# Attention that begins inside the layer norm, routing cut into pieces, pair rows staged from device memory

## The reference, cut to what matters

```python
# x: [4, 1024, 256] float32; 16 heads of 16; 8 experts, hidden 1024, top 2
xn = (x - mean(x)) / sqrt(var(x) + 1e-5)
q, k, v = xn @ W_q.T, xn @ W_k.T, xn @ W_v.T
decay[h, i, j] = gamma[h] ** (i - j) if i >= j else 0
attn = einsum('bihd,bjhd->bhij', q, k) * decay / sqrt(16)      # no softmax
y = einsum('bhij,bjhd->bihd', attn, v)
yn = (y - mean_h(y)) / sqrt(var_h(y) + eps)                    # over tokens and head dims
attn_out = (yn * gn_weight + gn_bias) @ W_o.T
probs = softmax(xn @ gate_w.T + gate_b)                        # [4096, 8]
val, idx = top_k(probs, 2)
ffn_out = sum_k val[k] * (relu(xn @ w1[idx[k]] + b1[idx[k]]) @ w2[idx[k]] + b2[idx[k]])
out = x + attn_out + ffn_out
```

## Time and profile before

| what | us |
|---|---|
| median of 3 runs | 790.35 |
| lowest, highest | 789.27, 793.92 |
| the profiled execution, its own time | 788.52 |
| its span, first to last instruction | 786.7 |
| first scores of attention in it | 61.6 |
| last round of attention in it ends near | 276 |

### The profile page before, as it was taken

How to read it: one execution, slowest core, us unless ns; L and a number is a source line. 1 busy time by engine, 2 the same in 40 slices (tenths; PEclk the granted TensorE clock), 3 DMA queues, 4 the chain that set the end, 5 groups by cost and what they waited for, 6 DMA issues and landing times.

```text
span 786.7 us, 20206 instructions
## 1 busy us (share of the span) xinstructions
PE 732.9 (93%) x6588; PEld 678.4 (86%) x6588; DVE 584.2 (74%) x1024; ACT 498.2 (63%) x880; POOL 283.1 (36%) x225
## 2 busy tenths in 40 slices
PE   2948999999999988999999999999999999999967
PEld 1426788888887788999999999999999999999957
DVE  6776777777777776877877878777778778778545
ACT  3832334333333386787787787887877877877780
POOL 0013333333334313344344354353353453443420
PEclk9977999999999998999999999999999999999988
DMA  9995333333334485788888888788888888886249
GB/s 294 371 335 176 119 105 108 98 103 101 101 101 136 157 299 150 227 218 252 213 232 251 206 236 257 184 250 242 208 247 239 213 249 227 217 252 173 35 109 332
DMA packets 89047, 157.85 MB, mean 201 GB/s; under 512 B 26496, under 2 KB 66560, under 8 KB 78976
## 3 DMA queue, kind: packets, MB, share of 16 engines
q1 hardware_dynamic: 74720, 138.87, 53.8%
q0 software_dynamic: 14304, 18.69, 14.5%
HBM read 111.67 MB, written 37.37 MB: 189 GB/s over the span
## 4 chain that ended last, share of the span: by engine, by line
PE 85%; DVE 5%; issue 4%; ACT 2%; DMA 2%; POOL 0%; SPq 0%; POOLq 0%; ACTq 0%; DVEq 0%; another core or an unknown queue 0%
PE ps L744 28%; PE ps L648 27%; PE ps L704 6%; PE ps L773 6%; PE ps L717 3%; PE ps L796 3%; PE ps L760 2%; PE ps L908 2%; PE ps L729 2%; PE ps L784 2%; PE ps L666 1%; PE ps L754 1%; PE ps L807 1%; ACT arena_f L539 1%; DMA xn<-x 1%
## 5 line engine op out<-in xcount | busy, mean ns | idle before, releaser
L648 PE MATMUL ps<-arena_r 128*128 128x256 f32 x1872 | 235.2, 286 | 2.2 <-DVE arena_r L1184 2.2
L744 PE MATMUL ps<-arena_r 128*128 128x256 f32 x1872 | 233.4, 285 | 1.9 <-DVE arena_r L1101 1.1
L744 PEld LDWEIGHTS ps<-arena_r 128*128 128x128 f32 x1872 | 229.5, 194 | 2.4 <-issue 2.4
L648 PEld LDWEIGHTS ps<-arena_r 128*128 128x128 f32 x1872 | 228.3, 193 | 2.4 <-issue 2.4
L444 POOL TENSOR_TENSOR fence_out<-eps_col 128x1 f32<-128x1 f32 x39 | 78.7, 2019 | 274.6 <-DVE arena_f L1160 274.6
L498 ACT ACTIVATE arena_r<-arena_f 128x2048 fp32r<-128x2048 f32 x77 | 143.7, 1921 | 0.0
L446 POOL DMA_INDIRECT sum_rows<-arena_f,pair_slot x78 | 122.7, 1574 | 18.1 <-issue 17.3
L580 ACT ACTIVATE arena_f<-ps,arena_f 128x256 f32<-128x256 f32 x156 | 65.3, 471 | 90.5 <-PE ps L744 79.5
L1176 DVE TENSOR_TENSOR arena_r<-arena_f,arena_r 128x2048 fp32r<-128x2048 f32 x39 | 89.4, 2292 | 38.7 <-ACT arena_r L498 38.7
L1184 DVE TENSOR_TENSOR arena_r<-arena_f,arena_r 128x512 fp32r<-128x512 f32 x78 | 55.9, 717 | 53.7 <-ACT arena_r L588 51.9
L1084 DVE TENSOR_TENSOR arena_f<-ps,cst 128x512 f32<-128x512 f32 x128 | 84.7, 683 | 14.9 <-PE ps L773 14.9
(11 more groups left out here) (134 smaller groups left out, 855.2 us busy)
## 6 DMA issues: line engine op xcount, KB each, us to landing
arena_f<-w SPq DMA_DIRECT2D x78, 1024.0 KB
xs_rows<-spare_rows SPq DMA_DIRECT2D x39, 258.0 KB, 3.6
arena_f<-xs_rows SPq DMA_DIRECT2D x39, 258.0 KB, 3.8
pair_chunk<-xn SPq DMA_DIRECT2D x32, 256.0 KB, 2.6
arena_f<-b SPq DMA_DIRECT2D x39, 128.0 KB, 4.0
xn<-x SPq DMA_DIRECT2D x8, 512.0 KB, 8.8
x_chunk<-xn SPq DMA_DIRECT2D x32, 128.0 KB
arena_f<-sum_rows SPq DMA_DIRECT2D x8, 512.0 KB, 7.6
```

The source lines that it names most:

```text
L648: last = pe.matmul(out_ap, lhs(a), rhs(b), start=start and n == 0, stop=stop and n == 2, **kw)
L744: last = pe.matmul(ps[:, H_BANK[hp], o * SLOT:(o + 1) * SLOT], w1_r[par][:, a, at:at + P], xs_r[:, b, k * SLOT:(k + 1) * SLOT], start=(m = ...
```

## The change

It has these parts.

1. **Loads.** SP loads group 0, the identity alone, group 1, gate weights, W_k and W_v, group 2, W_q, the other constants, groups 3 to 7, bias, W_o, gn.
2. **Layer norm.** Groups are normalised in place in `xn`: two tiles by VectorE, one by ScalarE, one by GpSimd; the copy back is gone. The gate's weights are padded to 32 columns so that the four tiles' logits go to four column blocks of TensorE (eight matmuls of 128 columns for two of 512), and one matmul brings a group's logits back. VectorE adds the bias once, for all groups, in round 0 of attention.
3. **Attention's head.** x_transposes(0) follow group 3, the first projections group 5. scores(0) no longer wait for routing.
4. **Routing in pieces.** VectorE does shifted_logits in round 1, and so on to experts_of_slots in round 11, each between new_state and the masked scores. The two counting matmuls are in round 5. Probabilities come from two exponentials and one sum. output_stats of the first rounds are left out there and done two a round in rounds 12 to 21.
5. **Pair rows.** SP writes each normalised group to `xn_rows` in device memory, with two spare-row writes between two groups; the other 25 spare rows follow three a round, the x copy in step 10. From step 11 on SP stages two tiles a step from `xn_rows`, with two DMAs each, into four buffers; the indirect DMAs read their rows from `rows2`. The first expert weights are issued in step 27. SP's and GpSimd's rounds are written out, without a loop. `y_t` waits for `xn_out` in place of a staging.

The diff, cut to its core:

```diff
@@ sync
             ln_load(0)
-            sp.dma_start(cst[:], const).then_inc(s["consts_in"], 16)
...
+            sp.dma_start(cst[:, 0:P], const[:, 0:P]).then_inc(s["ident_in"], 16)
+            ln_load(1)
+            sp.wait_ge(s["gate_zero"], 1)
...
+            weights_in(0)
+            ln_load(2)
+            weights_in(1)
+            sp.dma_start(cst[:, P:], const[:, P:]).then_inc(s["consts_in"], 16)
+            for g in range(3, NG):
+                ln_load(g)
...
+            def rows_out(g):
+                for name in ("ln_xn_v", "ln_xn_a", "ln_xn_p"):
+                    sp.wait_ge(s[name], g + 1)
+                sp.dma_start(xn_rows[:, g * GRP:(g + 1) * GRP, :], xn[:, g * GRP:(g + 1) * GRP, :]).then_inc(s["xn_out"], 16)
...
+            def pairs_stage(n):
+                b = n % NPB
+                wait(sp, s[f"scat{b}"], n // NPB * 32)
+                sp.dma_start(pair_chunk[b][:, :, 0:D], xn_rows[:, n:n + 1, :].to_broadcast([P, 2, D])).then_inc(s[f"rc{b}"], 16)
+                sp.dma_start(pair_chunk[b][:, :, D:W], pair_info[:, n]).then_inc(s[f"rc{b}"], 16)
+
+            rows_out(0)
             tokens_stage(0, 0)
             tokens_stage(1, 1)
             sp.wait_ge(s["spare"], 1)
...
+            for g in range(1, NG):
+                spare_out(2 * g - 2)
+                spare_out(2 * g - 1)
+                rows_out(g)
             sp.wait_ge(s["xt_psum"], 1)
             tokens_stage(2, 0)
...
+            def chunk_step(i):
+                if i + 3 < NT:
+
+                    sp.wait_ge(s["xt_psum"], i + 2)
+                    tokens_stage(i + 3, (i + 3) % 2)
+                for sl in range(2 * NG - 2 + 3 * i, min(2 * NG - 2 + 3 * i + 3, NS)):
+                    spare_out(sl)
+                if i == PAIRS_AT - 1:
+                    sp.dma_start(sum_rows[0:NT * P].rearrange("(p t) d -> p (t d)", p=P),
+                                 x.rearrange("b (q t) d -> (b q) (t d)", t=NT)).then_inc(s["sums_x"], 16)
+                if i == PAIRS_AT:
+                    sp.wait_ge(s["rows_done"], 2)
+                    sp.wait_ge(s["xn_out"], 16 * NG)
+                for n in range(2 * (i - PAIRS_AT), 2 * (i - PAIRS_AT) + 2):
+                    if 0 <= n < NT:
+                        pairs_stage(n)
+                if i == PAIRS_AT + NT // 2:
+                    sp.wait_ge(s["route_done"], 1)
+                    weights_load(0, 0)
@@ gpsimd
+            def ln_norm(g, par):
+                pool.wait_ge(s["ln_rstd"], g + 1)
+                nc.gpsimd.tensor_scalar(xn[:, g * GRP + 3], xn[:, g * GRP + 3], mean_var[:, par, 3, 0:1], rstd[:, par, 3:4],
+                                        ALU.subtract, ALU.mult).then_inc(s["ln_xn_p"], 1)
@@ scalar
+            ln_logit_copy(NG - 2, 0)
+            ln_copies(NG - 1, 1)
...
+            for i in range(COUNT_AT):
+                chunk(i, i % 2)
+
+            act.wait_ge(s["route"], 2)
             nc.scalar.activation(rt[2], rt[1], ACT.Exp).then_inc(s["route_exp"], 1)
+            nc.scalar.activation(rs[:, 6], rs[:, 5], ACT.Exp).then_inc(s["route_exp"], 1)
+            run_steps(act, COUNT_AT, NT, COUNT_AT + 1, 28, chunk)
@@ tensor
+            for g in range(NG):
+                ln_transposes(g, g % 2)
+                if g > 0:
+                    ln_logits(g - 1, (g - 1) % 2)
+                if g > 1:
+                    ln_back(g - 2, g % 2)
+                if g == 3:
+                    x_transposes(0, 0)
+                if g == 5:
+                    pe.wait_ge(s["w_split_h"], 2)
+                    pe.wait_ge(s["w_split_l"], 2)
+                    key_value_projection(0, 0)
+                    query_projection(0, 0)
+            ln_back(NG - 2, 0)
             key_transposes(0, 0)
+            query_transposes(0, 0)
             x_transposes(1, 1)
-            query_transposes(0, 0)
-            pe.wait_ge(s["rows_done"], 2)
+            ln_logits(NG - 1, 1)
             scores(0, 0)
             key_value_projection(1, 1)
...
+            run_steps(pe, 0, NT, COUNT_AT + 1, 28, chunk)
@@ vector
+            for g in range(-1, NG):
+                ln_step(g, g % 2)
+                if g == 2:
+                    tables()
+                if g == 4:
+                    tokens_low(0, 0)
+                if g == 6:
+                    keys(0, 0)
+                    queries(0, 0)
+            for i in range(LATE):
+                chunk(i, i % 2, stats=0, route=True)
+            run_steps(dve, LATE, 2 * LATE - 2, LATE, 2 * LATE - 2, lambda i, par: chunk(i, par, stats=2))
+            run_steps(dve, 2 * LATE - 2, NT, 2 * LATE - 2, 28, chunk)
```

More of the change, by code:

```diff
@@ L225, in build @@
         xs = ff(2, SJ, W)
+        pair_chunk += [xs[:, i] for i in range(2)]
         b1_slot = ff(2, FC)
@@ new lines, in first_expert, with next_peaks @@
+                chained(V.tensor_tensor(first, tmp, over_e(one), ALU.is_equal))
+                chained(V.scalar_tensor_tensor(rest, first, -BIG, logits[:], ALU.mult, ALU.add))
+            def next_peaks():
+                chained(V.tensor_reduce(next_peak, rest, AX, ALU.max))
+                V.tensor_tensor(gap, next_peak, peak, ALU.subtract).then_inc(s["route"], 1)
+                chained(V.tensor_tensor(tmp, rest, over_e(next_peak), ALU.is_equal))
+                chained(V.tensor_tensor(tmp, tmp, over_t(C["rank_low"]), ALU.mult))
@@ new lines, in second_expert, with read_counts @@
+            def second_expert():
+                chained(V.tensor_reduce(one, tmp, AX, ALU.max))
+                chained(V.tensor_tensor(second, tmp, over_e(one), ALU.is_equal))
+                V.tensor_tensor(mask_bf[:], first.rearrange("p t e -> p (t e)"), second.rearrange("p t e -> p (t e)"), ALU.add).then_inc(s["route_mask"], 1)
+            def read_counts():
+                dve.wait_ge(s["route_psum"], 1)
+                V.tensor_copy(by_expert, ps[:, NB - 1, 0:NT * E].rearrange("p (t e) -> p e t", t=NT)).then_inc(s["dve_route"], 1)
+                count[0] += 1
+                V.tensor_copy(counts_after, ps[:, NB - 1, NT * E:2 * NT * E].rearrange("p (t e) -> p t e", t=NT)).then_inc(s["route_read"], 1)
@@ new lines, in gate_values, with tokens_upto @@
+            def gate_values():
+                dve.wait_ge(s["route_exp"], 2)
+                chained(V.tensor_reduce(one, probs, AX, ALU.add))
+                chained(V.reciprocal(pair_info[:, :, 0, 1], one))
+                chained(V.tensor_tensor(pair_info[:, :, 1, 1], next_share, pair_info[:, :, 0, 1], ALU.mult))
+            def tokens_upto():
+                dve.wait_ge(s["dve_route"], count[0])
+                dve.wait_ge(s["ones"], 1)
+                chained(V.tensor_tensor_scan(upto.rearrange("p e t -> p (e t)"), ones_te,
+                                             by_expert.rearrange("p e t -> p (e t)"), 0.0, ALU.mult, ALU.add))
@@ L1131, in chunk @@
                     masked_scores(i, 3)
-            shifted_logits()
-            tokens_low(0, 0)
-            first_expert()
-            second_expert()
-            keys(0, 0)
-            queries(0, 0)
-            slots_of_experts()
-            gate_values()
-            rows_of_tokens()
-            experts_of_slots()
-            V.memset(state_f, 0.0).then_inc(s["st_f"], 1)
-            run_steps(dve, 0, NT, 4, 28, chunk)
+                if route and i == COUNT_AT:
+                    read_counts()
+            for g in range(-1, NG):
+                ln_step(g, g % 2)
+                if g == 2:
+                    tables()
+                if g == 4:
+                    tokens_low(0, 0)
[6 more added lines that the diff above has]
+            run_steps(dve, 2 * LATE - 2, NT, 2 * LATE - 2, 28, chunk)
             def ys_gated(sl, par):
```

329 lines of the change are left out of this document (169 added, 160 removed).

## The result

| | before | after |
|---|---|---|
| median of 10 runs each, us | 792.02 | 798.08 |
| lowest, highest | 789.27, 797.34 | 794.04, 806.35 |
| profiled execution, its own time / span | 788.52 / 786.7 | 797.52 / 795.6 |

A forecast was written before the change was run, and what follows sets the result against it. TensorE's own time was taken to bound the kernel, so only its holes could go. The terms, -24.9 - 0.6 + 4.5 + 0.6 + 1 - 1 = -20.4 us, gave 770.0 us against the median of 790.35, range 758 to 781.

The forecast's parts named there:

- Pair rows: Two tiles scattered a round in attention: 5.5 us of GpSimd in 6.44 us rounds, so nothing lost.
- Rival 3: GpSimd paces rounds 11 to 27, at 1.574 us an indirect DMA: +23 us, 793 us; chance 0.03.
- The start: Up to round 0's last projection: shorter layer norm, earlier scores, DMA queue deciding; gain 24.9 us (bounds 22 and 34).
- idle for x_chunk 2: In round 0 TensorE idles from about 35 to 42.5 us, until this token chunk lands through SP's queue.
- the cold restart: After idling in round 0, TensorE runs at half clock for 4.8 us; 3.3 us of work takes 5.7.
- rival 1: At the start x_chunk 2 lands before TensorE wants it, no idle, no cold restart: 761 us; chance 0.17.
- the landmark: Round 0's last projection (L704 before), forecast at 48.2 us where before has 73.09.
- Round 1: Attention's round after round 0: took 7.0 us before instead of 6.44, so 0.6 us more gain.
- Routing: Rounds 1 to 11: VectorE pieces of about 1.4 us, partly covered, cost +4.5 us (bounds 0 and 15).
- Rival 2: Routing pieces in attention's rounds have no cover: 15.4 us instead of 4.5, 781 us; chance 0.14.
- Code, loops: Written-out rounds and two VectorE loops in place of one mean code to be fetched: +1 us (bounds 0 and 3).
- The transition: End of attention: slot 0's weights issued about two rounds earlier, ahead of TensorE's loop exit: -1 us (bounds -2.6 and +1).

The follow-up runs named there:

- e1: The changed kernel without any pair row, staging and scatters both left out; 752.43 us against the changed kernel's 798.08.
- b1: The kernel before without its scatters, staging kept; 775.88 us against 791.08.
- e13: The changed kernel with four indirect DMAs a round, each released by a TensorE event, tiles staged a round ahead; median 768.43 us, ratio to before 0.9730.
- e2: The changed kernel with its staging DMAs kept and the scatters dropped; 751.48 us.
- e12: The changed kernel with four indirect DMAs a round, each released by a TensorE event, tiles staged a round ahead; 767.76 us in one execution.

## Why the prediction was wrong, point by point

- **Pair rows, which stand in the sum with nothing, were the step that failed.** The prediction compared GpSimd's 5.5 us of scatters with a round of 6.44 us and found room, and found the DMA engines below full. Both hold: GpSimd waited for staging, and DMA was half busy. But the fifteen rounds from 121.5 to 255.0 us took 133.5 us where 90 would do: 43.5 us lost. Without scatters (e1) the same rounds are 6.0 us. An operation that fits on its own engine was priced by that engine alone; its price to the others was in the trace of before, unread, but only as rounds of 6.44 us, which the prediction took for TensorE's own time. Without scatters b1 has 6.0: there lay the 15 us, and the sign that doubling them is not free.
- **Rival 3, slower at 793 us, 0.03,** named the right place and nearly the right time by a wrong mechanism. L473 stayed at 0.98 us, far below the 1.574 us that it needed. Its chance was set by the one price that could be checked, and nothing was put on scatters hurting others.
- **The start: -24.9 us forecast, -21.7 measured,** just below the bounds (22 to 34), and by a different path. The chain of after:

```profile
5.43 8.46 DMA xn<-x
...
21.21 1.36 POOL xn L441
...
29.59 1.35 POOL xn L441
...
37.56 1.36 POOL xn L441
...
42.55 0.41 PE ps L750 x2
...
43.54 1.15 PE ps L830 x16
```

  First scores at 43.54 us, not 31 to 35. GpSimd's normalisation of a tile, estimated at 0.6 us from a wider subtraction, takes 1.35 and is in the chain; two groups take 8 us where 5.1 were counted. TensorE, whose share was said to hide, is in the chain between them. VectorE's timeline shows how it got there:

```profile
19.14 2.09 DVE L1013 SCALAR_TENSOR_TENSOR ln_shift<-mean_var,rstd 128x4 f32<-128x4 f32 x1
...
27.27 0.42 DVE L1163 TENSOR_TENSOR arena_r<-ps,arena_r 128x256 fp32r<-128x256 f32 x1 [2.52 <-ACT arena_r L559]
...
36.24 0.42 DVE L1170 TENSOR_TENSOR arena_f<-ps,cst 128x256 f32<-128x256 f32 x1 [3.12 <-PE ps L759]
```

  tokens_low (L1163) and keys (L1170) now stand between layer-norm groups in VectorE's list and wait 2.52 us for the first transposes and 3.12 us for the first projection; the prediction counted only the time that they are busy. Where no such wait lies between, two groups' statistics are 2.7 us apart (27.61 and 30.33), near the 2.56 of the forecast. And L1013, elsewhere 0.16 us long, took 2.09 beside GpSimd's splitting of a weight (L447, 18.79 to 21.21 us): there VectorE paid for all of it, not for half. VectorE was through at 38.4 us, where 28.6 to 33 were forecast.

  So there was no idle for x_chunk 2: L750 waits for no DMA. DMA share fell from 0.98 to 0.45 at 40 us, close to the 42.5 us worked out for the queue's end, but it bound nothing. The clock stood at 1.00 from 40 to 50 us, so the cold restart didn't come either. This is rival 1's condition without its time. A late layer norm and a wait that never came partly cancelled, so it is luck that the landmark, passed at 51.3 us, came so near the 48.2 of the forecast.
- **Round 1, -0.6 us:** not there. The 7.0 us were read up to a row of L1084; by the projections' starts before takes 6.0 us (73.0 to 79.0) and after 6.3, with the routing piece.
- **Routing: right in size, over rounds of 6.0 us.** Forecast +4.5 us for eleven rounds and +0.6 for the counts. Measured 51.3 to 121.5 us, 70.2 us, against 66 for eleven of 6.0: +4.2 for both. The piece of round 1 in the chain of after costs VectorE 1.45 us (50.82 to 52.27), where 1.4 was worked out, and about 1 us of it is covered. Rival 2 (10.9 us more) falls. Against before's 71.4 us the stretch even gained 1.2, since the scatters had left these rounds; the forecast, which adds to before's rounds of 6.44 us, has no term for that.

```profile
50.82 0.34 DVE rs L1063
51.18 0.43 DVE arena_f L1064
51.64 0.44 DVE arena_f L1066
```

- **Code, loops: +1 us.** e1, with all the written-out rounds, has 6.0 us rounds from round 12 on; nothing was paid there.
- **The transition, -1 us:** the distance of 8.9 us near the end of before's loop is gone in after (6.0 each). A gain of the size forecast or a little more, but by luck: it was put down to the weights and the loop's exit, and b1, with both in place and no scatters, has 6.0 there as well. It was the last two tiles in a row.
- **The expert phase:** equal; after is 9.8 us behind at the last projection and 8.9 at the end.
- **The sum in measured stretches:** -21.7 for the start, -1.2 for the eleven rounds with routing, +32.7 for the eighteen with scatters, -0.9 for the rest: +8.9 us of span, where -20.4 was forecast.

With e13 the forecast's sum comes true, 768.4 us against 770.0, but not by its terms: pacing takes back 30 of the 43.5 us, and the 13 that stay are about what before pays for its 32 tiles too (16 us in 28 rounds), which the forecast's rounds of 6.44 us held unseen. That the two times agree is luck.

## What to carry to other kernels

An operation that leaves its own engine idle time may still be dear to the others: measure a settled round with it taken out (6.0 against 6.44 us here) before doubling it. Indirect DMAs of GpSimd should be spread over a round, with a short break after each tile's pair, and released late enough that the data have been staged, so that the release and not the data sets the moment. When the chain of waits says "unknown", lay the timelines of all engines beside one another and see which of them is the only one at work.

## What the runs showed of the hardware that was not expected

Back-to-back indirect DMAs on GpSimd's queue held up TensorE, VectorE and ScalarE: 0.2 to 0.6 us for one tile (two indirect DMAs), 2.1 for two in a row, 9.2 for four, 15.5 for six, some 40 for fifteen, with the DMA engines about half busy (0.57 in 120 to 140 us of after) and with 8 bytes a row as with whole rows. The Trainium skill, SBUF — State Buffer, section Who interferes with whom, says that DMA never contends with a compute engine. Its sentence is on ports, and staging in e2 agrees with it (751.48 us with it, 752.43 without); for indirect DMAs in a row the measurements decide otherwise, whatever the place where they meet.

The long holes also cost the clock: granted 0.87 and 0.79 in 120 to 140 and 140 to 160 us of after, 1.00 in e1 and e12 there.
